# The opening of a fused two-layer kernel in halves of x, and its gate steps one by one

## What is computed

```python
mod = (_silu(L0_c) @ L0_wmod).reshape(L0_c.shape[0], 6, 1, -1)
sa, ca, ga, sb, cb, gb = (mod[:, 0], mod[:, 1], mod[:, 2], mod[:, 3], mod[:, 4], mod[:, 5])
ga = (2 * (ga >= 0) - 1) * jnp.maximum(jnp.abs(ga), 0.25)
gb = (2 * (gb >= 0) - 1) * jnp.maximum(jnp.abs(gb), 0.25)
h = _layernorm(x, axis=-1) * (1 + ca) + sa
x = x + ga * _L0_attn_ref(h, L0_attn_Wqkv, L0_attn_Wo)
```

## Time and profile before

| what | us |
|---|---|
| median of three runs | 783.2 (782.8 to 784.45) |
| the profiled execution's own time | 783.09 |
| span of its trace | 781.3 |
| PE busy | 720.8 |
| DVE busy | 553.2 |
| ACT busy | 443.6 |
| POOL busy | 379.7 |

### The profile page before, as it was taken

How to read it: one execution, slowest core, us unless ns; L and a number is a source line. 1 busy time by engine, 2 the same in 40 slices (tenths; PEclk the granted TensorE clock), 3 DMA queues, 4 the chain that set the end, 5 groups by cost and what they waited for, 6 DMA issues and landing times. The chain is left out here.

```text
span 781.3 us, 12361 instructions
## 1 busy us (share of the span) xinstructions
PE 720.8 (92%) x4372; PEld 622.1 (80%) x4372; DVE 553.2 (71%) x1257; ACT 443.6 (57%) x915; POOL 379.7 (49%) x410
## 2 busy tenths in 40 slices
PE   5797999999999999999999799999979999889997
PEld 4576888888888888888887689997768778567787
DVE  3466777677776776768777688777578888566666
ACT  3464666666666666666666343322678776546432
POOL 5792586536865368643451330002656554204773
PEclk9998999999999999999999999999999999999999
DMA  7000000000000000004000040003100000000001
GB/s 248 4 11 8 14 16 15 13 8 14 10 20 14 8 15 8 13 15 170 7 8 8 1 135 1 1 1 115 49 0 2 1 1 1 0 3 1 1 1 55
DMA packets 19083, 19.85 MB, mean 25 GB/s; under 512 B 2126, under 2 KB 16974, under 8 KB 19022
## 3 DMA queue, kind: packets, MB, share of 16 engines
q1 hardware_dynamic: 18206, 18.41, 7.4%
q10 hardware_dynamic: 816, 0.66, 0.3%
HBM read 18.01 MB, written 1.05 MB: 24 GB/s over the span
## 5 line engine op out<-in xcount | busy, mean ns | idle before, releaser
L880 POOL TENSOR_TENSOR at_swapped<-at_swapped,at_sin 128x512 f32<-128x512 f32 x40 | 51.6, 1289 | 134.3 <-ACT at_swapped L603 134.3
L625 ACT ACTIVATE at_probs<-at_probs,at_negmax 128x128 f32<-128x128 f32 (+7 forms) x128 | 99.6, 778 | 29.4 <-DVE at_negmax L709 27.5
L709 DVE CUSTOM_DVE_ANT_0 at_probs<-at_scores,causal 128x128 f32<-128x128 f32 (+7 forms) x128 | 96.2, 751 | 16.9 <-PE at_scores L59 16.2
L518 PE MATMUL at_turn<-ident_sb,at_probs 128*128 128x128 f32 x576 | 86.4, 278 | 15.0 <-DVE at_full_T_lo L725 13.9
L518 PEld LDWEIGHTS at_turn<-ident_sb,at_probs 128*128 128x128 f32 x576 | 67.5, 142 | 23.8 <-issue 11.7
L618 ACT ACTIVATE at_edge_T_hi<-at_turn 128x128 fp32r<-128x128 f32 (+3 forms) x128 | 55.5, 434 | 34.8 <-PE at_turn L518 34.4
L57 PE MATMUL at_scores<-at_kT_hi,room 128*128 128x512 f32 (+1 forms) x192 | 66.6, 347 | 4.5 <-DVE at_v L691 3.5
L618 ACT ACTIVATE at_full_T_hi<-at_turn 128x512 fp32r<-128x512 f32 x64 | 38.3, 598 | 50.4 <-PE at_turn L518 48.4
L58 PE MATMUL at_scores<-at_kT_lo,room 128*128 128x512 f32 (+1 forms) x192 | 66.7, 347 | 0.0
L59 PE MATMUL at_scores<-at_kT_hi,room 128*128 128x512 f32 (+1 forms) x192 | 66.4, 346 | 0.0
L725 DVE TENSOR_TENSOR at_edge_T_lo<-at_turn,at_edge_T_hi 128x128 fp32r<-128x128 f32 (+3 forms) x128 | 61.4, 480 | 1.4 <-ACT at_edge_T_hi L618 1.0
(11 more groups left out here) (395 smaller groups left out, 2289.9 us busy)
## 6 DMA issues: line engine op xcount, KB each, us to landing
at_wq_in<-L_attn_Wqkv SPq DMA_DIRECT2D x16, 128.0 KB, 2.2
at_wo_in<-L_attn_Wo SPq DMA_DIRECT2D x16, 128.0 KB, 2.0
staging<-L_ffn_routed_w SPq DMA_DIRECT2D x7, 256.0 KB, 4.7
ff_wmod<-L_wmod SPq DMA_DIRECT2D x1, 1536.0 KB, 6.5
at_wmod<-L_wmod SPq DMA_DIRECT2D x1, 1024.0 KB, 8.3
staging<-L_ffn_w_gate SPq DMA_DIRECT2D x1, 1024.0 KB, 5.2
staging<-L_ffn_w_up SPq DMA_DIRECT2D x1, 1024.0 KB, 7.3
staging<-L_ffn_w_down SPq DMA_DIRECT2D x1, 1024.0 KB, 9.7
```

The costliest lines, as they stand in the source:

```text
L518: mm = pe.transpose(p_turn[t % 2][:, b - b0, :], probs[:, s % 4, b * P:(b + 1) * P], m.ident[:, :])
L625: act.activation(row, row, ACT.Exp, scale=-1.0, bias=negmax[:, unit % 4:unit % 4 + 1], accum_out=rowsum[:, unit // NT % 2, i:i + 1])\
L709: dve.tensor_tensor_reduce(out=probs[:, s % 4, 0:width], in0=p_scores[s % 2][:, 0:width], in1=m.causal[:, S - width:], scale=-1.0, scalar= ...
L880: turning = pool.tensor_tensor(swapped[:, r % 2, :], swapped[:, r % 2, :], sin[:, cols], ALU.mult)
```

## The change

x is loaded in four pieces of two tiles, two on each queue, and each half of x has its own measurements, root and norms: tiles 0 to 3 are normalised on DVE, tiles 4 to 7 on ACT with the bias `nbias`. The c vectors move to the ACT queue; identity and mask are issued there behind the first activation. `hi` of the key and query weights is made on ACT, `lo` on the Pool behind the first norms; of the value weights `hi` is made on the Pool and `lo` on DVE. Of each half's second quarter ACT makes `hi` (`rows_hi`) and DVE `lo` (`low_rows`). PE warms up on a zeroed tile with 5 products before anything is loaded, projects keys and queries of the first half and one value tile before it turns the second half, and makes value tiles 1 to 3 ahead of the second keys and queries; ACT and DVE follow that order. The ten gate operations are placed one in a unit: the first gate in units 4 to 8, the second in 17 to 21. All later waits on the root's counter are one higher.

```diff
+        p_gates, p_col = score_banks[2], [turn_banks[0][:, 0:4], score_banks[3][:, 0:4]]
+        row_banks = score_banks[0:2] + turn_banks
+        GATE_UNITS = (4, 17)
-        POOL_TILES = (2, 3, 6, 7)
...
-                sp.dma_start(m.x[:, 0:4, :], a["L0_attn_x"].rearrange("o (n p) d -> p (o n) d", p=P)[:, 0:4, :]).then_inc(x_in[0], 16)
-                for n in range(2):
-                    sp.dma_start(craw[:, n, :], a[f"L{n}_c"]).then_inc(c_in, 16)
+                for half in range(2):
+                    sp.dma_start(m.x[:, 4 * half:4 * half + 2, :], x_rows[:, 4 * half:4 * half + 2, :]).then_inc(x_in[half], 16)
...
@@ PE @@
+                pe.wait_ge(zeros_done, 1)
+                keep_warm(pe, early_banks[1], m.causal, 5)
                 pe.wait_ge(wmod_in[0], 16)
                 pe.wait_ge(c_silu, 1)
                 mod_columns(0)
-                keep_warm(pe, early_banks[1], wmod[:, 0, :], 3)
                 pe.wait_ge(const_in, 32)
                 turn_x(0)
                 turn_x(1)
                 gate_rows()
+                key_job(0, 0, early_banks[0])
+                query_job(0, 0, early_banks[1])
+                mod_columns(6)
+                value_job(0)
+                pe.wait_ge(col_done, 1)
                 turn_x(2)
                 turn_x(3)
-                key_job(0, 0, early_banks[0])
-                query_job(0, 0, early_banks[1])
-                pe.wait_ge(rows_read, 1)
-                mod_columns(6)
+                value_job(1)
+                value_job(2)
+                value_job(3)
                 key_job(0, 1, early_banks[2])
-                pe.wait_ge(col_done, 2)
                 query_job(0, 1, early_banks[3])
-                for t in range(4):
-                    value_job(t)
@@ ACT @@
-                act.dma_start(m.x[:, 4:8, :], a["L0_attn_x"].rearrange("o (n p) d -> p (o n) d", p=P)[:, 4:8, :]).then_inc(x_in[1], 16)
+                act.dma_start(craw[:, 0, :], a["L0_c"]).then_inc(c_in, 16)
+                for half in range(2):
+                    act.dma_start(m.x[:, 4 * half + 2:4 * half + 4, :], x_rows[:, 4 * half + 2:4 * half + 4, :]).then_inc(x_in[half], 16)
+                act.dma_start(craw[:, 1, :], a["L1_c"]).then_inc(c_in, 16)
+                act.wait_ge(c_in, 32)
+                act.activation(m.csil[:, :, :], craw[:, :, :], ACT.Silu).then_inc(c_silu, 1)
                 act.dma_start(m.ident[:, :], a["ident"]).then_inc(const_in, 16)
                 act.dma_start(m.causal[:, S - P:], a["mask"]).then_inc(const_in, 16)
-                act.wait_ge(c_in, 32)
-                act.activation(m.csil[:, :, :], craw[:, :, :], ACT.Silu).then_inc(c_silu, 1)
-                variance_roots(act, m, range(NT), 1)
-                act.wait_ge(const_in, 32)
-                load_table(act, m, ACT.Exp, 0)
-                for n in range(4):
-                    scale_shift(n)
+                variance_roots(act, m, FIRST_TILES, 1)
+                act.wait_ge(wk_loaded, 16)
+                act.activation(wk.hi, wk_in[:, :, :], ACT.Copy).then_inc(wk_hi, 1)
+                act.wait_ge(wq_loaded, 16)
+                act.activation(wq.hi, wq_in[:, :, :], ACT.Copy).then_inc(wk_hi, 1)
+                scale_shift(0)
+                scale_shift(1)
+                variance_roots(act, m, LAST_TILES, 2)
+                rows_hi(1)
                 act.wait_ge(rows_mm, 1)
                 act.activation(m.gate[:, 0, :, :], p_gates.rearrange("p (g d) -> p g d", d=DM), ACT.Copy).then_inc(rows_read, 1)
                 copy_rope(0, early_banks[0])
+                act.wait_ge(rstd_done, 1)
+                for n in LAST_TILES:
+                    act.activation(xn[:, n, :], m.x[:, n, :], ACT.Identity, scale=m.rstd[:, n:n + 1], bias=m.nbias[:, n:n + 1]).then_inc(act_normed, 1)
                 copy_rope(1, early_banks[1])
+                scale_shift(2)
+                scale_shift(3)
+                rows_hi(3)
+                load_table(act, m, ACT.Exp, 0)
+                for t in range(4):
+                    value_hi(t)
                 copy_rope(2, early_banks[2])
                 copy_rope(3, early_banks[3])
-                for t in range(4):
-                    value_hi(t)
@@ DVE @@
-                    if unit == 5:
-                        gates()
+                    for n, start in enumerate(GATE_UNITS):
+                        if start <= unit < start + 5:
+                            gate_step(n, unit - start)
...
-                for n in range(NT):
-                    dve.wait_ge(x_in[n // 4], 16)
-                    chain.step(dve.bn_stats(m.stats[:, n, :], m.x[:, n, :]))
-                variances(dve, m, chain, range(NT))
+                dve.wait_ge(x_in[0], 32)
+                tile_stats(FIRST_TILES)
+                variances(dve, m, chain, FIRST_TILES)
+                dve.wait_ge(x_in[1], 32)
+                tile_stats(range(4, 5))
+                inverse_roots(dve, m, chain, FIRST_TILES, 1)
+                for n in FIRST_TILES:
+                    dve.tensor_scalar(xn[:, n, :], m.x[:, n, :], m.meanvar[:, n, 0:1], m.rstd[:, n:n + 1],
+                                      ALU.subtract, ALU.mult).then_inc(normed, 1)
                 columns(1)
-                inverse_roots(dve, m, chain, range(NT), 1)
-                dve.nop(nofuse=True).then_inc(rstd_done, 1)
-                for n in range(NT):
-                    if n not in POOL_TILES:
-                        dve.tensor_scalar(xn[:, n, :], m.x[:, n, :], m.meanvar[:, n, 0:1], m.rstd[:, n:n + 1],
-                                          ALU.subtract, ALU.mult).then_inc(normed, 1)
-                for n in range(4):
-                    split_rows(n)
-                columns(2)
+                tile_stats(range(5, NT))
+                variances(dve, m, chain, LAST_TILES)
+                split_rows(0)
+                low_rows(1)
+                inverse_roots(dve, m, chain, LAST_TILES, 2)
+                spread(dve, m, LAST_TILES).then_inc(rstd_done, 1)
+                dve.wait_ge(wv_hi, 1)
+                dve.tensor_tensor(wv.lo, wv_in[:, :, :], as_f32(wv.hi), ALU.subtract).then_inc(wv_ready, 1)
                 dve.wait_ge(tables_in[0], 32)
                 cos_rope(0, 0, early_banks[0], proj_free)
+                columns(2)
                 cos_rope(1, 0, early_banks[1], query_free)
+                split_rows(2)
+                low_rows(3)
+                for t in range(4):
+                    value_lo(t)
                 dve.wait_ge(tables_in[1], 32)
                 cos_rope(2, 1, early_banks[2], proj_free)
                 cos_rope(3, 1, early_banks[3], query_free)
-                for t in range(4):
-                    value_lo(t)
@@ POOL @@
-                split_k(0)
-                split_q(0)
-                pool.wait_ge(rstd_done, 1)
-                for n in POOL_TILES:
-                    pool.tensor_scalar(xn[:, n, :], m.x[:, n, :], m.meanvar[:, n, 0:1], m.rstd[:, n:n + 1], ALU.subtract, ALU.mult).then_inc(pool_normed, 1)
+                for n, (staged, out, ready) in enumerate(((wk_in, wk, wk_ready), (wq_in, wq, wq_ready))):
+                    pool.wait_ge(wk_hi, n + 1)
+                    pool.wait_ge(normed, 4)
+                    pool.tensor_tensor(out.lo, staged[:, :, :], as_f32(out.hi), ALU.subtract).then_inc(ready, 1)
                 pool.wait_ge(wv_loaded, 16)
-                split_weights(wv_in[:, :, :], wv, wv_ready)
+                pool.tensor_scalar(wv.hi, wv_in[:, :, :], 1.0, 1.0, ALU.mult, ALU.mult).then_inc(wv_hi, 1)
```

More of the change, by code:

```diff
@@ L314, in attention0 @@
         turn_banks = [p_turn[n][:, :, :].rearrange("p a b -> p (a b)") for n in range(2)]
-        p_gates, p_col = turn_banks[1], [turn_banks[n][:, 0:4] for n in range(2)]
+        p_gates, p_col = score_banks[2], [turn_banks[0][:, 0:4], score_banks[3][:, 0:4]]
+        row_banks = score_banks[0:2] + turn_banks
         early_banks = [p_proj[:, :], p_att[:, :], turn_banks[0], turn_banks[1]]
@@ L783, in columns, with gate_step @@
                     dve.tensor_scalar(done[:, 2:4], done[:, 2:4], 1.0, None, ALU.add).then_inc(col_done, 1)
-                def gates():
-                    dve.wait_ge(rows_read, 1)
-                    for n in range(2):
-                        out = m.gate[:, 0, n, :]
-                        chain.run(dve.tensor_scalar(sgn[:, :], out, 0.0, 2.0, ALU.is_ge, ALU.mult))
-                        chain.run(dve.tensor_scalar(sgn[:, :], sgn[:, :], -1.0, None, ALU.add))
-                        chain.run(dve.tensor_tensor(out, out, sgn[:, :], ALU.mult))
-                        chain.run(dve.tensor_scalar(out, out, 0.25, None, ALU.max))
-                        dve.tensor_tensor(out, out, sgn[:, :], ALU.mult).then_inc(gates_done, 1)
+                def gate_step(n, step):
+                    out = m.gate[:, 0, n, :]
+                    chain.settle()
+                    if step == 0:
+                        dve.wait_ge(rows_read, 1)
```

(21 more changed lines are left out.)

48 lines of the change are left out of this document (31 added, 17 removed).

## The result

| | before | after |
|---|---|---|
| median, five runs each | 784.45 us (782.8 to 787.11) | 778.28 us (777.08 to 778.79) |
| ratio after / before | | 0.9908, 95% interval 0.9888 to 0.9927 |
| span of the trace | 781.3 | 776.7 |
| profiled execution | 783.09 | 778.5 |

The kernel is faster, and its time lies in the range (770.5 to 778.5), at its slow end and 4.1 us above the forecast of 774.2. Two sizes of the gain stand beside each other: 4.6 us by the spans, 7.2 by the ratio (0.0092 of 784.45; the interval is 5.7 to 8.8). The kernel before scatters over 4.3 us and its profiled execution was one of its shorter ones.

A forecast was written before the change was run, and what follows sets the result against it. PE waits in the opening, where the Pool's rotation chain stands 0.5 us behind it, and around DVE's block of gate steps. Opening 5.9 + first gate 3.3 - second gate 0.2 = 9.0 us, giving 774.2 us; range 770.5 to 778.5.

The forecast's parts named there:

- the slack of 0.4: End of the Pool's rotation chain, 0.5 us ahead of the ScalarE query copy: no longer ahead, 0.4 us earlier.
- The cosine wait: Pool's rotation chain in the opening: its wait for the Vector engine's cosine product goes, 1.5 us earlier.
- no change: Rival: PE, not the Pool, set the query copy, and a dropping clock eats the gates' gain; 783 us, chance 0.05.
- slower: Rival: a gate step at unit 17 holds DVE and PE for up to 14 us; 793 us, chance 0.05.
- The term of the lock, 1.8: Opening: the second half's split falls into the Pool's uninterrupted work and holds its chain up, 1.8 us back.
- I take 12.8 for the start of `turn_x(0)`, since its queue is empty by then.: Opening: PE's first transpose at 12.8, late bound 14.3 for the mask; part of the key product's 5.8 us gain.
- Another 0.3: Opening: PE's transposes and part of the gate rows run at the slower rate, costing 0.3 us.
- Opening values: I count nothing.: Opening: values ahead of second keys and queries no longer hold the first scores (3.51 us idle), counted as nothing.
- first gate: net 3.3: Units 4 to 8: removing the gate block gives 6.0 us, less the first five steps' cost; net 3.3, bounds 1.5 and 4.5.
- The other five go to units 17 to 21, where PE is the bound: 0.2 back (0 to 1.8).: Second gate's five steps, placed where PE is the bound, cost 0.2 us, from 0 to 1.8.
- lock stronger: Rival: opening splits and gate steps wait for whole Pool operations; 2 to 7 us gained, 778.2 us, chance 0.22.
- my own signs of failure: Fourth rotation ending after 44, first root after 11.5, gate steps over 1 us each, or PE idling in units 17 to 21.

The follow-up runs named there:

- values last: The changed kernel with value tiles 1 to 3 behind the second keys and queries again; 778.85 us, ratio 0.9926 to the kernel before.
- loads first: The changed kernel with both c loads, the x pieces, identity and mask all issued before ScalarE waits for c; 775.24 us, ratio 0.9888.
- the last kernel: Loads first, second gate in gaps and no lock together, with second keys and queries ahead of value tiles 2 and 3; 771.53 us, ratio 0.9826.
- no lock: The changed kernel with the scaled quarters of x's second half left in PSUM, where casts and subtractions read them; 777.51 us, ratio 0.9902.
- No second gate: The changed kernel without the second gate's five steps in units 17 to 21, so the output differs; 775.75 us, ratio 0.9880.
- second gate in gaps: The changed kernel with the second gate's steps in units 9, 17, 41, 49 and 73, ahead of the key's cosine product; 775.39 us, ratio 0.9877.
- gates alone: The kernel before with only the gate steps moved to units 4 to 8 and 17 to 21; 781.82 us, ratio 0.9955.
- opening alone: The changed kernel with the gate block back in one piece behind unit 5; 780.06 us, ratio 0.9936.
- both: The changed kernel with loads first and second gate in gaps together; 773.32 us, ratio 0.9849.
- first gate early: Second gate in gaps, with the first gate's five steps moved into the opening behind the value weights' split on DVE; 775.00 us, ratio 0.9879.

## Why the prediction was right in its time and wrong in its terms

**What held.** The Pool's chain of rotations, not PE, sets the end of the opening. In the eleven kernels with the new opening other than values last, the lead at unit 2 is what the end of the fourth rotation moved, plus the slack of 0.4: 1.77 and 2.16 in after, 5.77 and 6.16 in loads first, 6.51 and 6.90 in the last kernel. The cosine wait is gone (1.5), the copy of head 1's query follows the fourth rotation directly (0.4 of slack, measured 0.39), the block of gate steps was worth taking apart, and "no change" and "slower" did not come about. The term of the lock, 1.8, was measured as 1.9: the chain without the cosine wait took 20.06 us before and 21.95 after. Its make-up was not what I said, though: 0.8 is lock (the second rotation took 5.60 instead of 4.80), 0.86 the wait for PE's second query product, the rest small gaps. Lock and wait cover each other: in no lock the chain took 21.94.

**"I take 12.8 for the start of `turn_x(0)`, since its queue is empty by then."** This step failed. The first transpose started at 15.19. The mask was issued at 9.29, not 8.0, because c landed at 8.9 and not 7.0; and it took 5.8 us although nothing but the identity stood ahead of it in its own queue. The DMA engines were fully busy until 14 with the other queue's loads; that this is the cause is argued, since no run takes those loads away. The number was there to be read: in the kernel before, the same load took 5.8 too. I had a late bound of 14.3 and took an early value in front of it for the empty queue. Loads first, which issues the mask at 3.18, puts the transposes at 12.82: 2.4 us.

**"Another 0.3" for the slower rate.** Mis-sized. From transposes to first rotation I reckoned 7.0 us and measured 8.25, and 6.63 and 5.94 in the two kernels whose clock stayed up: the lower clock costs 1.6 to 2.3. I had looked at 1-column products to guess the rate, and not at the warm-up products that the change takes away ahead of the transposes. With four more of them in that place (warm longer) the clock stayed up. The two errors, 2.4 and 1.25, are the whole of the opening's shortfall (5.8 less 2.14).

**"Opening values: I count nothing."** Wrong in the other direction: 1.5 to 2.2 us by the trace of values last, 0.6 by its median. The early values keep PE at work while DVE splits, and with that its clock up. Without them the chain would have been held up longer, so my 1.8 was right only with this order.

**Gate steps, first gate: net 3.3, measured 4.5.** Mis-sized by 1.2, on the safe side. The first step took 1.40 and cost 1.3 by itself; from unit 5 to 12 the lead then grew 5.8, which is the block of 6.0 less what the other four steps cost. So either these four cost 0.2 instead of about 2, or the block was worth more than 6.0; this stays open, because the one run without steps there had the clock at its lower level beside it. TensorE's granted clock is 1.00 from 66 to 74 in after, so the block's slow stretch is gone as forecast.

**"The other five go to units 17 to 21, where PE is the bound: 0.2 back (0 to 1.8)."** This step failed, beyond its bound: 2.5. A share of PE near 99% over 50 us does not say that the engine behind it has room just there. In units 17 to 21 a step waited for a Pool operation (0.64, 1.14, 0.78), the maximum and the addition to `x` stood behind the step, and PE, which needed that addition, stopped for 1.70. No second gate and second gate in gaps show that the steps and nothing else are the cause.

The time landed inside the range by luck, 0.2 us from its edge, because the errors have both signs: 3.7 too much from the opening, 1.2 too little from the first gate, 2.3 too much from the second; 9.0 so becomes the lead of 4.2, and the span another 0.4 behind the last unit compared. By time the "lock stronger" rival (778.2) came out, by mechanism it did not. Of my own signs of failure three are there: fourth rotation after 44 (45.39), steps over 1 us, PE idle in unit 20.

**What stays open.** The ratio gives 2.6 us more than the traces. The kernels with the old opening spread most (before 3.3 to 4.8 us within a series, gates alone 2.9, opening alone 0.7), so part of the new opening's gain may be that something in the old one is late in most executions and was not in the profiled one. With one trace of each kernel this can't be shown; values last, with the new opening, also spread 2.6.

## What to carry to other kernels

An empty queue is no argument that a load lands soon: read from the trace before what the same load took, and the DMA share of the stretch, and issue small loads that somebody needs first early, not behind an activation. An operation on the Vector engine that works from SBUF to SBUF beside a busy Pool belongs in a gap where the Vector engine waits anyway; ahead of the operation that paces PE it can bring most of a Pool operation's wait with it (1.14 instead of 0.41), even where PE's busy share is 99%. Before moving warm-up products away, look at what idle time they fill. A long wait of PE costs twice, once itself and once in the clock behind it, so cost what follows it at the lower rate.

## What the runs showed of the hardware

- Loads of the same size went at different speeds by queue: x pieces of 256 KB landed 3.3 us after their issue on SP's queue and 5.5 on ScalarE's, and 6.7 there in loads first. Identity and mask (64 KB each), issued at about 9 us with nothing else ahead of them, took 5.4 and 5.8; issued at about 3 us, 6.1 and 6.9; in the kernel before, issued at 1.2 and 1.8, 5.3 and 5.8.
- TensorE after a wait: granted clock 0.50 after 4.02 us idle; products at the lower rate after 2.80 and 0.68 in values last, with three at the full rate between; full speed after 2.00 us in loads first; the lower rate from the first transpose after 2.60 in both, and only from the gate rows on (3.16 instead of 1.89) after 2.27 in the last kernel. Idle time alone doesn't tell: in first gate early it was 0.50 from 50 to 54 where PE had waited no more than 1.3 us at a time. It came back at moments that differed by more than 1 us between executions of nearly the same opening (gate rows 2.52 and 3.62).
- Vector and Pool held each other up on both sides with their operands in SBUF (3.37 for two subtractions of 0.69; 1.56 for a Pool addition of 1.29), and not at all with one operand of the subtraction in PSUM. A single step lost anything from nothing to 1.1 us.
- A table load on ScalarE took 1.28 us with the next instruction right behind it (9.77 to 11.07).
